# Regrouping a pair's TensorE work by tile shape in a fused attention and expert kernel, with the keys projected two pairs ahead

## The reference

```python
q, k, v = x @ Wq, x @ Wk, x @ Wv              # 16 heads of 64; q and k then get rotary embedding
sim  = q @ k.T / 8, causal mask
attn = softmax(sim)
x1   = layernorm(x + (attn @ v) @ Wo + bo)
w    = softmax(x1 @ gate.T + bias), the best 2 of 8 experts, scaled to sum 1
y    = sum over the 2 experts of w[e] * (gelu(x1 @ up[e].T) @ down[e].T)      # inner width 512
out  = layernorm(layernorm(y) + x1)
```

## Time and profile before

| | |
|---|---|
| median of 3 runs | 871.32 us |
| profiled execution, its own time | 873.04 us |
| its span | 871.3 us |
| granted TensorE clock, mean of the span | 0.983 |
| TensorE busy | 827.4 us (95%) |
| VectorE busy | 691.2 us (79%) |
| ScalarE busy | 627.2 us (72%) |
| GpSimd busy | 567.1 us (65%) |

### The profile page before, as it was taken

The page is one execution under the profiler, slowest core; times in us unless marked ns, Lnnn a source line. Parts: engine busy times, 40 slices in busy tenths (PEclk is TensorE's granted clock), DMA queues, the critical chain, the costliest instruction groups (busy, mean ns, idle before and its releaser), DMA issues.

```text
span 871.3 us, 21016 instructions
## 1 busy us (share of the span) xinstructions
PE 827.4 (95%) x6238; PEld 577.6 (66%) x6238; DVE 691.2 (79%) x2696; ACT 627.2 (72%) x1674; POOL 567.1 (65%) x587
## 2 busy tenths in 40 slices
PE   7999999999999999999999999999999899999950
PEld 3555666666666666666666666666666599999950
DVE  5687797989898989897989798979888866433595
ACT  3777787788777877777787778777777756565643
POOL 4576656456755765576567655765576368999883
PEclk9999999999999999999999999999999999999985
DMA  5011101001100100010001000100021232322624
GB/s 157 32 37 38 53 20 32 16 14 29 34 25 14 50 13 26 13 49 14 26 13 49 14 25 14 50 16 14 19 67 60 62 95 77 81 74 78 197 81 121
DMA packets 52414, 41.43 MB, mean 48 GB/s; under 512 B 6096, under 2 KB 46160, under 8 KB 52304
## 3 DMA queue, kind: packets, MB, share of 16 engines
q1 hardware_dynamic: 47952, 31.11, 13.1%
q0 software_dynamic: 4352, 8.99, 2.9%
HBM read 23.74 MB, written 12.14 MB: 41 GB/s over the span
## 4 chain that ended last, share of the span: by engine, by line
PE 88%; DVE 6%; issue 2%; ACT 1%; POOL 1%; DMA 0%; POOLq 0%; SPq 0%; DVEq 0%; ACTq 0%
PE SB L804 16%; PE OB L836 16%; PE TB L823 13%; PE SB L848 8%; PE SB L962 6%; PE SB L823 3%; PE TB L971 3%; PE OB L971 3%; PE AB L793 3%; PE OB L730 2%; PE OB L731 1%; PE OB L732 1%; PE AB L732 1%; PE AB L730 1%; PE AB L731 1%
## 5 line engine op out<-in xcount | busy, mean ns | idle before, releaser
L1048 ACT ACTIVATE Pr_all<-Sm,nmax 128x512 f32<-128x512 f32 (+3 forms) x512 | 282.2, 557 | 70.1 <-DVE nmax L1221 69.0
L1221 DVE CUSTOM_DVE_ANT_0 Sm<-SB,causal 128x512 f32<-128x512 f32 (+3 forms) x512 | 219.8, 485 | 46.6 <-PE SB L804 46.4
L521 POOL TENSOR_TENSOR shared<-shared,sin_t 128x512 f32<-128x512 f32 x63 | 80.7, 1281 | 171.5 <-DVE shared L1201 171.5
L1239 DVE SCALAR_TENSOR_TENSOR x_acc<-SB,rinv,x_acc 128x128 f32<-128x128 f32 x512 | 144.2, 344 | 40.1 <-PE SB L848 33.6
L1060 ACT ACTIVATE PT<-TB 128x1024 f32<-128x1024 f32 (+2 forms) x192 | 135.0, 738 | 52.6 <-PE TB L823 52.6
L804 PE MATMUL SB<-kT,qT 64*128 64x512 f32 (+3 forms) x1024 | 166.6, 444 | 0.4 <-issue 0.4
L836 PE MATMUL OB<-PT,shared 128*64 128x128 f32 (+3 forms) x1024 | 152.6, 439 | 0.1
L823 PEld LDWEIGHTS TB<-ident,Pr_all 128*128 128x128 f32 x1024 | 113.9, 141 | 57.6 <-ACT Pr_all L1048 47.8
L823 PE MATMUL TB<-ident,Pr_all 128*128 128x128 f32 x1024 | 136.7, 277 | 1.4 <-issue 1.0
L804 PEld LDWEIGHTS SB<-kT,qT 64*128 64x128 f32 x1024 | 77.9, 187 | 69.9 <-issue 53.4
L513 POOL TENSOR_TENSOR shared<-shared,sin_t 128x512 f32<-128x512 f32 x64 | 81.6, 1276 | 53.0 <-DVE shared L1195 51.6
(11 more groups left out here) (297 smaller groups left out, 1451.5 us busy)
## 6 DMA issues: line engine op xcount, KB each, us to landing
wo<-in_wo SPq DMA_DIRECT2D x64, 64.0 KB, 1.8
PT<-yrows SPq DMA_DIRECT2D x7, 512.0 KB
xt<-xrows SPq DMA_DIRECT2D x40, 65.0 KB
x_acc<-in_x SPq DMA_DIRECT2D x8, 256.0 KB, 3.0
wdown<-in_wdown SPq DMA_DIRECT2D x8, 256.0 KB, 3.1
pay<-pay SPq DMA_DIRECT2D x8, 256.0 KB
x_acc<-pay SPq DMA_DIRECT2D x8, 256.0 KB
shared<-in_wup SPq DMA_DIRECT2D x8, 256.0 KB, 2.7
```

The lines of the kernel that those rows point to most:

```text
L521: nc.gpsimd.tensor_tensor(k_rot, k_rot, sin_t[:, :], ALU.mult).then_inc(k_mul, 1)
L1048: nc.scalar.activation(Pr[j][:, 0:n], Sm[j], ACT.Exp, bias=nmax[:, j:j + 1], scale=-1.0, accum_out=rsum[p][:, h * QB + qb:h * QB + qb + 1] ...
L1221: nc.vector.tensor_tensor_reduce(out=Sm[j], in0=SB[2 * (group % 2) + h][:, at:at + n], in1=causal[:, T - n:T], scale=-0.125, scalar=HUGE, ...
L1239: last = nc.vector.scalar_tensor_tensor(out=tile, in0=SB[2 + h][:, i * P:i * P + P], scalar=rinv[:, h * QB + i:h * QB + i + 1], in1=tile, ...
```

## The change

TensorE's order in unit u becomes: scores group 0 of u, output projection of u-2, scores groups 1 and 2 of u (all 64x128); transposes group 0 of u-1, K of u+2, V block, transposes group 1 of u-1, Q of u+2, transposes group 2 of u-1, routing work (all 128x128); attend u-1 (128x64). The array changes its tile shape three times in a unit. K is projected two units ahead, as Q was. The output projection goes to AB and OB, the result of attend to the first bank of TB, K to AB, V and Q to OB, the routing work to the second bank of TB. ScalarE and VectorE are put in the order that this gives. VectorE does its routing work at the end of a unit, after both rotary steps. After the 64 units a longer tail finishes the last two of them. The diff, cut to its core:

```diff
+        AO = ps("AO", (P, 2, 512))
+        AB, OB = AO[:, 0, :], AO[:, 1, :]
...
+        def o_bank(u):
+            return OB if u == UNITS - 1 else TB[:, 0, :]
+
+        def y_bank(u):
+            return (SB[2], SB[3]) if u == UNITS - 1 else (AB, OB)
+
+        def wide(u):
+            return AO if UNITS - 3 <= u < UNITS - 1 else TB
...
@@ GpSimd, attention @@
-                if not last:
-                    rotate_k(u + 1, 1 - p)
...
+                if u + 2 < UNITS:
+                    rotate_k(u + 2, p)
                     rotate_q(u + 2, p)
...
@@ TensorE, project_q @@
+                elif 2 < u <= VBLOCKS - QB + 2:
+
+                    pe.wait_ge(v_ready, QB + u - 2)
                 elif u > 2:
-
-                    bank = OB
-                    pe.wait_ge(o_ready, u - 2)
+                    pe.wait_ge(y_read, 2 * (u - 3))
...
@@ TensorE, project_k @@
+                elif u > 3:
+                    pe.wait_ge(y_read, 2 * (u - 4) + 1)
...
@@ TensorE, project_v @@
-                    bank = AB[:, :]
-                    pe.wait_ge(k_read, block - QB + 2)
+                    bank = OB
+                    u = block - QB + 1
+                    if u == 1:
+                        pe.wait_ge(q_read, 3)
+                    else:
+                        pe.wait_ge(y_read, 2 * (u - 1))
...
@@ TensorE, transpose @@
+                if group == 0:
+                    wait(pe, o_ready, u)
+                elif group == 2:
+
+                    pe.wait_ge(maxed, min(BLK * (u + 1) + DONE_BY[1], BLK * UNITS))
+                elif wide(u) is TB:
+
+                    pe.wait_ge(pt_ready, 3 * u + 1)
                 else:
+                    pe.wait_ge(y_read, 2 * u)
+                    if u == UNITS - 2:
+                        pe.wait_ge(tables_ready, 1)
...
@@ TensorE, attend @@
+                pe.wait_ge(pt_ready, 3 * u + 2)
...
                 for kb in reversed(range(QB)):
-                    if kb > 0:
-
-                        pe.wait_ge(pt_ready, 3 * u + QB - kb)
+                    if kb == 1:
+
+                        pe.wait_ge(pt_ready, 3 * u + 3)
...
@@ TensorE, project_out @@
+                    pe.wait_ge(k_read, min(u + 4, UNITS))
+                    pe.wait_ge(q_read, min(u + 4, UNITS))
...
@@ TensorE, bank_free @@
-                    ab_free(u + 1)
+                    pe.wait_ge(pt_ready, 3 * (u - 1) + 2)
...
@@ TensorE, attention @@
                 score(u, p, 0)
...
+                if u >= 2:
+                    project_out(u - 2, p)
+                    pe.wait_ge(pt_ready, 3 * (u - 1))
...
                 score(u, p, 1)
                 pe.wait_ge(maxed, BLK * u + DONE_BY[0])
                 score(u, p, 2)
...
+                if not first:
+                    transpose(u - 1, 1 - p, 0)
+                if u + 2 < UNITS:
+                    project_k(u + 2, *second)
+                if last:
+                    turn_places(0, AB)
+                if 1 <= u <= VBLOCKS - QB:
+                    project_v(QB + u - 1)
+                if not first:
+                    transpose(u - 1, 1 - p, 1)
+                if u + 2 < UNITS:
                     project_q(u + 2, *second)
+                if not first:
+                    transpose(u - 1, 1 - p, 2)
...
                 if not first:
-                    pe.wait_ge(maxed, BLK * u + DONE_BY[1])
-                    project_out(u - 1, 1 - p)
+                    attend(u - 1, 1 - p)
...
@@ TensorE, after attention_units @@
+            project_out(u - 1, 0)
+            transpose(u, 1, 0)
+            pe.wait_ge(y_read, 2 * u - 1)
             transpose_x(0)
+            transpose(u, 1, 1)
+            transpose(u, 1, 2)
+            up(0)
+            pe.wait_ge(pt_ready, 3 * u + 2)
             transpose_x(1)
+            attend(u, 1)
             transpose_x(2)
             project_out(u, 1)
...
@@ ScalarE, attention @@
+                if u >= 2:
+                    copy_o(u - 2, p)
+                if not first:
+                    for j in range(2, BLK):
+                        exp(u - 1, 1 - p, j)
...
+                if not first:
+                    copy_pt(u - 1, 1 - p, 0)
+                if 1 <= u <= VBLOCKS - QB:
+                    copy_v(QB + u - 1)
+                if not first:
                     copy_pt(u - 1, 1 - p, 1)
                     copy_pt(u - 1, 1 - p, 2)
                 exp(u, p, 0)
                 exp(u, p, 1)
...
@@ VectorE, attention @@
                     rope_q(1)
+                    rope_k(1)
...
                 mask_max(u, 0)
                 mask_max(u, 1)
+                if u >= 2:
+                    scale_y(u - 2, p)
...
+                for j in range(2, 6):
+                    mask_max(u, j)
+                if u + 2 < UNITS:
+                    rope_k(u + 2)
+                mask_max(u, 6)
+                mask_max(u, 7)
+                if first:
+                    add_bias(0)
+                if u + 2 < UNITS:
+                    rope_q(u + 2)
...
+                if n == BIAS_AT and not last_batch(batch):
+                    add_bias(batch + 1)
...
```

More of the change, by code:

```diff
@@ L645, in attention @@
                     send_row(batch - 2, 2 * n + 1)
-                if not (last_batch(batch) and n >= PAIRS - 2):
+                if n == SPLIT_AT and not last_batch(batch):
+                    split_x(batch, u)
+                if u + 2 < UNITS:
+                    rotate_k(u + 2, p)
                     rotate_q(u + 2, p)
@@ L663, in _ @@
             rotate_q(1, 1)
+            rotate_k(1, 1)
             attention_units(attention)
@@ L741, in project_q @@
                     pe.wait_ge(x_split, batch)
-                bank = AB
+            def project_q(u, n, batch):
+                inputs_ready(n, batch)
+                bank = AB if u < 2 else OB
                 if u == 1:
@@ L847, in project_out @@
                         half = slice(D * h, D * h + D)
-                        last = nc.tensor.matmul(SB[2 + h][:, i * P:i * P + P], OT[p][half, i * P:i * P + P],
+                        last = nc.tensor.matmul(y_bank(u)[h][:, i * P:i * P + P], OT[p][half, i * P:i * P + P],
                                                 wo[p][half, :], start=True, stop=True)
@@ L1076, in attention @@
                         copy_v(block, v_bank(block))
-                else:
+                if u >= 2:
[3 more added lines that the diff above has]
+                        exp(u - 1, 1 - p, j)
+                if n == HIGH_AT and not last_batch(batch):
+                    act.wait_ge(x_next_in, 16 * (batch + 1))
+                    wait(act, q_proj, PAIRS * batch)
+                    nc.scalar.activation(x_hi[(batch + 1) % 2][:, :], x_next[:, :], ACT.Copy).then_inc(x_high, 1)
+                if batch > 0 and n == PICK_AT:
+                    exp_logits(batch - 1)
+                if not first:
[3 more added lines that the diff above has]
+                if not first:
                     copy_pt(u - 1, 1 - p, 1)
@@ L1081, in attention @@
                 exp(u, p, 1)
-                if not first:
-                    copy_o(u - 1, 1 - p)
-                if n == HIGH_AT and not last_batch(batch):
-                    act.wait_ge(x_next_in, 16 * (batch + 1))
-                    wait(act, k_proj, PAIRS * batch)
-                    nc.scalar.activation(x_hi[(batch + 1) % 2][:, :], x_next[:, :], ACT.Copy).then_inc(x_high, 1)
-                exp(u, p, 2)
-                if u < VBLOCKS - QB:
-                    copy_v(QB + u)
-                exp(u, p, 3)
-                exp(u, p, 4)
-                copy_pt(u, p, 0)
-                exp(u, p, 5)
-                exp(u, p, 6)
-                exp(u, p, 7)
-                if batch > 0 and n == PICK_AT:
-                    exp_logits(batch - 1)
             attention_units(attention)
-            u = UNITS - 1
-            for group in (1, 2):
-                copy_pt(u, 1, group)
             def copy_xT(t):
@@ L1114, in gelu @@
                 nc.scalar.activation(hT[t % 3][:, :], HB[t % 3][:, :], ACT.Gelu).then_inc(gelu_done, 1)
+            u = UNITS - 1
+            copy_o(u - 1, 0)
+            for j in range(2, BLK):
+                exp(u, 1, j)
+            copy_pt(u, 1, 0)
             copy_xT(0)
-            copy_o(u, 1)
+            copy_pt(u, 1, 1)
+            copy_pt(u, 1, 2)
             copy_xT(1)
@@ L1120, in _ @@
             gelu(0)
+            copy_o(u, 1)
             copy_xT(2)
```

146 lines of the change are left out of this document (56 added, 90 removed).

## The result

The kernel after takes **924.08 us** (922.76 to 924.89, 4 runs), the kernel before 871.18 us: a ratio of **1.061**, interval [1.059, 1.063]. It is 53 us slower, where 873 us was forecast and the range ended at 881.

A forecast was written before the change was run, and what follows sets the result against it. TensorE bounds the kernel; its 0.42 us a unit saved is given back by a VectorE and ScalarE loop. Units -3.3, start -2.6, end +7.4 make +1.5 us on the median 871.3: 873 us, range 857 to 881.

The forecast's parts named there:

- The edges: Changes of TensorE's tile shape: some 0.21 us per run, so three runs instead of five save 0.42 us a unit.
- the rival that the change doesn't do what it says: Edge cost belongs to first weight loads after waits, not the shape: about 880 us, counted within slower's 0.23.
- What is late next: Plain unit's loop through VectorE and ScalarE: V waits for scale_y, attend for transposes 1's copy; 10.40 us against 10.37.
- its last link: Attend in a plain unit waits for the copy of transposes 1; its second wait, for transposes 2's copy, costs 0.07 us.
- faster in part: Rival: VectorE's chain some 0.2 us shorter, plain unit 10.15 to 10.25 us, kernel 858 to 864 us; chance 0.27.
- The edges of the whole: Kernel's start and end: start 2.6 us ahead, tail 39.1 us where before 31.7, 7.4 behind.
- the paragraph on VectorE: VectorE's waiting, about 2.2 us a plain unit, just holds routing work of 1.3 to 2.5 us; costed at nothing.
- VectorE ends last around n = 1 to 3: Rival: routing work makes next first mask late, 0.4 us in three units of 7 batches, +8 us, 881; slower's chance 0.23.

The follow-up runs named there:

- e5: e4 with scores group 2 moved between transposes group 0 and K, five runs of one tile shape a unit instead of three: 884.87 us.
- e4: e1 with the reciprocal of the softmax sums taken ahead of mask 0 instead of between mask 1 and the multiply-adds: 865.39 us.
- e6: e4 with the two transposes of query block 0 moved from group 1 to group 2: 884.85 us.
- e1: Kernel after, with VectorE's routing work and bias put between masks 5 and 6, ahead of its rotary steps: 875.28 us.
- e2: Kernel after, order untouched, GpSimd rotating only 64 of 512 columns of Q and K from unit 2 on: 874.62 us.
- e7: e6 with batch 0's bias addition in unit 1 instead of unit 0: 883.9 us.
- e8: e4 with batch 0's bias addition moved from unit 0 to unit 1, ahead of the rotation of K: 864.39 us.
- e9: e4 with GpSimd rotating only 64 of 512 columns of Q and K from unit 2 on: 866.25 us.

## Why the prediction was wrong

**The edges: right.** Three runs instead of five save about 0.4 us of TensorE's own time. e5 puts two runs back and pays 0.39 us a unit, so the rival that the change doesn't do what it says falls: the cost belongs to the shape.

**What is late next: right but for its last link.** The loop of first mask, second mask, reciprocal, multiply-adds, V, transposes, copy and attend was laid out to 10.40 us; it measured 10.36 to 10.37. V started at 4.97 for 5.01. Units 2 to 5 took 10.75 (10.65), units 6 to 8 10.53 to 10.58 (10.57), n = 4 11.33 (11.35). e4 shortens the loop by 0.2 and the unit becomes 10.19 (10.15): what was the bound for "faster in part" is the loop with V on time. The last link was wrong. Attend waits for the last copy, 1.7 us ahead of the next unit; I had put that at 0.07 of waiting and given the bound to the copy of transposes 1 (e6). Both copies follow V by the same TensorE work in this order, so the sum came out all the same; in this link that was luck.

**The edges of the whole: nearly right.** Scores 1 of unit 2 came at 35.20 (35.05). From scores 1 of unit 61 to the end of the last projection it was 41.8 us (39.1 forecast), and 40.0 in e1.

**The failed step** is this one of the paragraph on VectorE: about 2.2 us of waiting a plain unit, "and routing work of 1.3 to 2.5: just enough, so nothing". The slack was about right. The work was priced at durations of operations that had run while GpSimd stood idle, and moved to where GpSimd works. Nine operations and their gaps had cost 1.7 us; in their new place three of them took 1.0 to 1.2 each and the nine 4.6. The forecast asked of moved work which queues and banks it meets, and not which neighbour on the same SBUF ports. The rival "VectorE ends last around n = 1 to 3" had the mechanism (a late mask 0, with `scale_y`, V and all behind it) and the units n = 2 and 3, but a price of 0.4 us where 1.4 and 2.4 were measured; it rested in part on the x1 copy with the bias, whose lateness would show at n = 4 and cost nothing there (11.33 for 11.35); and it left out the picks and the placing, half of the 7.15 us a batch. It said +8 us, and the term is 49 (e1 and e2), some 2.6 of it, in the profiled execution, by way of the clock.

The kernel before had a hint. The bias addition reads two operands from SBUF, and it took 1654 ns on the mean there, against 688 in e1, in these two rows of before and of e1:

```profile
L1255 DVE TENSOR_TENSOR x_acc<-x_acc,bo_t 128x512 f32<-128x512 f32 x6 | 9.9, 1654 | 0.0
```

```profile
L1290 DVE TENSOR_TENSOR x_acc<-x_acc,bo_t 128x512 f32<-128x512 f32 x6 | 4.1, 688 | 0.0
```

The same instruction in two durations in one kernel, or over twice what its columns take elsewhere (a mask of 512 columns takes 0.69), is a sign of a neighbour. The bias was the one piece that already stood beside GpSimd's rotations.

**The sum without this step.** With the lock out of the way and all else as in the change, e1 and e2 give 875.3 and 874.6 us in a job where the kernel before took 1.5 us more than in the forecast's runs. 873 us was the right sum of its other terms, and the change, even so, brings nothing: the saving of 0.42 us a unit on TensorE goes into V's wait. Half of it comes back only with the reciprocal's move.

## What to carry to other kernels

When a change moves small VectorE operations, look at GpSimd's timeline at the new place: one with two SBUF operands, of four columns or 512, is held until GpSimd's operation ends. Put such work where GpSimd is idle, and let reductions and operations with a PSUM operand, which the rows show untouched, lie beside it. A long VectorE operation with two SBUF operands also holds up GpSimd. And after grouping work on the bounding engine, walk the chain through the other engines: what was cover for a copy (e6) or a reciprocal (e4) before is now on the path.

## What the runs showed of the hardware

- A VectorE operation of 128x4 that takes 0.16 us alone takes 0.98 to 1.19 beside GpSimd's `tensor_tensor` of 512 columns (1.27). TENSOR_TENSOR and SCALAR_TENSOR_TENSOR with both operands in SBUF are stopped, and some operations with one SBUF input: a TENSOR_SCALAR (170 to 1178 ns), a COPY (168 to 989) and a CAST (172 to 1067) of 4 or 8 columns, means of before and after. The reductions are not (185 and 186), nor are `scale_y`'s multiply-adds, with one operand in PSUM: eight take 2.29 us at 412.11, beside four GpSimd operations from 410.79 to 413.91, and 2.29 at 399.33, with GpSimd idle.
- GpSimd is no slower for the short operations (the rotations at 405.76, 407.00 and 408.41 take 1.27 or 1.28), but it is for the bias addition of 512 columns. One of its multiplications, in the kernel after, starts while the addition runs and takes 1.73:

```profile
418.86 1.51 DVE L1290 TENSOR_TENSOR x_acc<-x_acc,bo_t 128x512 f32<-128x512 f32 x1
```

```profile
419.77 1.73 POOL L526 TENSOR_TENSOR shared<-shared,sin_t 128x512 f32<-128x512 f32 x1
```

  Of the 64 of L526 the longest is 1.73 after and 1.29 in e1, where the addition stands elsewhere.
- One more run of another matmul shape costs 0.2 us (e5), both ends together.
- TensorE's granted clock was 0.79 from 20 to 36 us in the profiled executions of e1 and e4, 0.89 in e6 and e7, and 1.00 in those of after, e2, e5, e8 and e9. From 24 to 28 us it was 0.50 in e1 and e4, the lower level (1.2 GHz). Just before unit 1's scores (near 21.8 us) TensorE had stood still for 1.90 to 2.02 us in the first four and for 1.32 to 1.70 in the others. But the seven waits of 2.04 to 2.05 us in the n = 3 units of the kernel after were followed by a fall only twice, with a mean clock of 0.88 in these two units. What decides is open.
